# Attention kernel: the sums of two tiles in one run, three buffers of probabilities, one buffer of rounded biases

## What is computed

```python
qkv = (x.reshape(B, S, dim) @ qkv_w + qkv_b)            # x is _gn(x)
attn = jnp.einsum('bqc,bkc->bqk', q * scale, k)
rel_h = jnp.einsum('bhwc,hkc->bhwk', r_q, Rh)
rel_w = jnp.einsum('bhwc,wkc->bhwk', r_q, Rw)
attn = attn + rel_h[..., :, None] + rel_w[..., None, :]  # 2304 x 2304 for each head
out = softmax(attn) @ v
x = x + (out @ proj_w + proj_b)
```

## Time and profile before

| | us |
|---|---|
| median of 3 runs | 7006.76 |
| range of the runs | 7003.55 to 7010.83 |
| the profiled execution, its own time | 7003.42 |
| its span, first to last instruction | 7001.6 |
| PE busy | 6841.4 (98%) |
| DVE busy | 5486.4 (78%) |
| ACT busy | 4650.1 (66%) |
| GpSimd busy | 934.5 (13%) |

### The profile page before, as it was taken

One profiled execution on the slowest core, in us unless ns is written; L12 is line 12 of the kernel. 1 busy time (PEld: TensorE's weight loads), 2 busy tenths in 40 slices (PEclk: granted clock), 3 DMA queues, 4 the chain that ended last, 5 costly groups with the idle time before them and its releaser, 6 DMA issues.

```text
span 7001.6 us, 139199 instructions
## 1 busy us (share of the span) xinstructions
PE 6841.4 (98%) x53600; PEld 4298.1 (61%) x53600; DVE 5486.4 (78%) x10165; ACT 4650.1 (66%) x10033; POOL 934.5 (13%) x967
## 2 busy tenths in 40 slices
PE   7999999999999999999999999999999999999998
PEld 4666666666666666666665666656666566666664
DVE  6887888778887788877888778887787878877883
ACT  2667676666666676666766666667676666766765
POOL 2112010110102110111111111102101121101110
PEclk8999999999999999999999999999999999999999
DMA  5666676666667666666666666766667666666663
GB/s 142 142 148 155 134 150 144 155 154 133 152 133 158 149 138 154 142 162 138 145 143 147 153 142 141 153 146 154 143 139 152 139 159 142 139 148 144 144 145 93
DMA packets 306306, 1013.72 MB, mean 145 GB/s; under 512 B 107440, under 2 KB 196976, under 8 KB 215920
## 3 DMA queue, kind: packets, MB, share of 16 engines
q1 hardware_dynamic: 305648, 1004.81, 64.4%
HBM read 745.26 MB, written 255.69 MB: 143 GB/s over the span
## 4 chain that ended last, share of the span: by engine, by line
PE 93%; DMA 3%; DVE 2%; issue 0%; SPq 0%; ACT 0%; POOL 0%; POOLq 0%; DVEq 0%; ACTq 0%
PE work L791 31%; PE work L782 27%; PE work L861 26%; PE work L807 4%; DMA moving<-rel_scratch 3%; PE work L826 2%; PE work L845 2%; DVE mpart L660 1%; PE work L834 1%; PE work L813 0%; DMA qk_scratch<-back 0%; DVE xb L651 0%; ACT probs L547 0%; DVE stats L610 0%; POOL back L495 0%
## 5 line engine op out<-in xcount | busy, mean ns | idle before, releaser
L660 DVE TENSOR_REDUCE mpart<-work 128x1 f32<-128x512 f32 (+1 forms) x8640 | 5091.4, 631 | 1217.2 <-PE work L791 1196.8
L547 ACT ACTIVATE probs<-work 128x512 f32<-128x512 f32 (+1 forms) x8640 | 4047.8, 557 | 951.4 <-PE work L782 936.8
L782 PE MATMUL work<-moving,keys 113*128 113x512 f32 (+1 forms) x8640 | 3395.8, 394 | 78.8 <-DMA moving<-rel_scratch 73.7
L791 PE MATMUL work<-mkeys,hi 128*128 128x512 f32 (+1 forms) x8640 | 3451.7, 401 | 11.8 <-DVE mpart L660 8.6
L791 PEld LDWEIGHTS work<-mkeys,hi 128*128 128x128 f32 x8640 | 1647.8, 191 | 1152.4 <-DVE mpart L660 866.8
L861 PE MATMUL work<-probs,vall 128*17 128x288 f32 x27648 | 2016.3, 409 | 0.0
L782 PEld LDWEIGHTS work<-moving,keys 113*128 113x128 f32 x8640 | 1645.7, 191 | 534.4 <-ACT probs L547 141.4
L861 PEld LDWEIGHTS work<-probs,vall 128*17 128x17 f32 x27648 | 637.4, 97 | 803.2 <-ACT probs L547 245.0
L480 POOL TENSOR_TENSOR full<-full,hi 128x384 f32<-128x384 f32 x576 | 580.8, 1009 | 1417.0 <-DVE hi L705 1417.0
L530 ACT ACTIVATE full<-work 48x384 f32<-48x384 f32 x576 | 279.3, 486 | 604.5 <-PE work L807 604.5
L535 ACT ACTIVATE full<-work 48x384 f32<-48x384 f32 x576 | 278.9, 484 | 583.6 <-PE work L807 583.6
(11 more groups left out here) (42 smaller groups left out, 649.1 us busy)
## 6 DMA issues: line engine op xcount, KB each, us to landing
moving<-rel_scratch SPq DMA_DIRECT2D x1728, 144.0 KB
moving<-qk_scratch SPq DMA_DIRECT2D x288, 576.0 KB
rel_scratch<-hi SPq DMA_DIRECT2D x192, 432.0 KB, 5.9
rel_scratch<-full SPq DMA_DIRECT2D x192, 432.0 KB, 5.5
moving<-rel_scratch SPq DMA_DIRECT2D x288, 288.0 KB
image<-qk_scratch SPq DMA_DIRECT2D x384, 144.0 KB, 4.2
keys<-qk_scratch SPq DMA_DIRECT2D x192, 288.0 KB, 4.8
qk_scratch<-split_hi SPq DMA_DIRECT2D x144, 192.0 KB, 3.8
```

Of the source, the lines that this page charges most:

```text
L547: act.activation(probs[:, tile % RING, lo:up], bank[:, 0:up - lo], ACT.Exp).then_inc(act_read, 1)
L660: dve.tensor_reduce(mpart[:, u % 2, q, m:m + 1], bank[:, 0:MSPLIT[m][1] - MSPLIT[m][0]], AX.X, ALU.max)\
L782: pe.matmul(bank[:, 0:up - lo], tile_of(keys[0:K_ROWS, u % 2, :], c, third), moving[0:K_ROWS, slot_of(u, third)[0], lo:up], start=True, st ...
L791: pe.matmul(bank[:, 0:up - lo], hi[:, u % 2, q * P:(q + 1) * P], mkeys[:, u % 2, lo:up], start=True, stop=True).then_inc(for_dve, 1)
```

## The change

The sums of tiles are no longer one run at the end of each tile: at the end of every even t PE does those of the two tiles before, one behind the other, and at the end of odd t none. So that the exponentials of a further tile have a place, `probs` has three buffers in place of two. The space comes from `hi`, which has one buffer in place of two. A conversion of `hi` may therefore overwrite columns only after the maxima matmuls that read them; each now waits for the last reduction of those, and the sixth moves from t = 13 after the third reduction to the end of t = 13, ahead of `top`. On SP the store of `hi` moves from t = 13 to t = 14, and that of `full` from t = 14 to t = 15.

```diff
-RING = 2
+RING = 3
...
-        hi = sb("hi", [P, 2, N], F32R)
+        hi = sb("hi", [P, N], F32R)
...
-                    if t == 13 and u + 2 < UNITS:
-                        sp.wait_ge(hi_ready, NB * (u + 3))
-                        rel_store(u + 2, hi[:, (u + 2) % 2, :].bitcast(F32), 0, rel_hi_stored)
                     if t == 14 and 0 <= u + 1 < UNITS:
                         top_load(u + 1, 0)
                     if t == 14 and u + 2 < UNITS:
-                        sp.wait_ge(lo_ready, NB * (u + 3))
-                        rel_store(u + 2, full[:, :], 1, rel_lo_stored)
+                        sp.wait_ge(hi_ready, NB * (u + 3))
+                        rel_store(u + 2, hi[:, :].bitcast(F32), 0, rel_hi_stored)
...
                     if t == 15 and 0 <= u + 1 < UNITS:
                         top_load(u + 1, 1)
+                    if t == 15 and u + 2 < UNITS:
+                        sp.wait_ge(lo_ready, NB * (u + 3))
+                        rel_store(u + 2, full[:, :], 1, rel_lo_stored)
...
                 if r == 0:
                     dve.wait_ge(fullq_in, 32 * (u + 1))
-                    if u >= 2:
-                        dve.wait_ge(rel_hi_stored, 32 * (u - 1))
-                dve.tensor_copy(hi[:, u % 2, cols], full[:, cols]).then_inc(hi_ready, 1)
+                    if u:
+                        dve.wait_ge(rel_hi_stored, 32 * u)
+                if u:
+                    dve.wait_ge(dve_read, place["max", u - 1, 3 * r + 2, MAXB - 1] + 1)
+                dve.tensor_copy(hi[:, cols], full[:, cols]).then_inc(hi_ready, 1)
...
-                        if 8 <= t < 14 and i == 2 and -2 <= u and u + 2 < UNITS:
-                            high(u + 2, t - 8)
+                        if -2 <= u and u + 2 < UNITS:
+                            if 8 <= t < 13 and i == 2:
+                                high(u + 2, t - 8)
+                            if (t, i) == (13, 5):
+                                high(u + 2, 5)
...
-                        if i == SB and 0 < tile <= TILES * UNITS:
+                        if i == SB and t % 2 == 0 and 0 < tile <= TILES * UNITS:
+                            attend(tile - 2)
                             attend(tile - 1)
```

More of the change, by code:

```diff
@@ L479, in low @@
                 pool.wait_ge(hi_ready, NB * u + r + 1)
-                pool.tensor_tensor(full[:, cols], full[:, cols], hi[:, u % 2, cols].bitcast(F32), ALU.subtract)\
+                pool.tensor_tensor(full[:, cols], full[:, cols], hi[:, cols].bitcast(F32), ALU.subtract)\
                     .then_inc(lo_ready, 1)
@@ L790, in fill @@
                         pe.wait_ge(mkeys_in[u % 2], 32 * (u // 2 + 1))
-                    pe.matmul(bank[:, 0:up - lo], hi[:, u % 2, q * P:(q + 1) * P], mkeys[:, u % 2, lo:up],
+                    pe.matmul(bank[:, 0:up - lo], hi[:, q * P:(q + 1) * P], mkeys[:, u % 2, lo:up],
                               start=True, stop=True).then_inc(for_dve, 1)
```

## The result

The changed kernel takes 7193.09 us (median of four runs, 7190.21 to 7196.79). The kernel before takes 7005.4 us (four runs, 7003.55 to 7010.83). The ratio is 1.0268, 95% interval 1.0255 to 1.028. The prediction was 7077 us with a range up to 7160: it foresaw a loss of 74 us, and the loss is 188 us, above the range. The mechanism it names (three banks, DVE late in the first tile of a pair, PE waiting in the second) is there, in pairs 11-12 and 15-16 of plain units to the hundredth of a microsecond. What failed is what it took for pairs with other work in them, above all the projection and value items; and a term that it set at nothing is there.

A forecast was written before the change was run, and what follows sets the result against it. PE, busy for 98%, bounds the kernel; its possible 259 us saving is outweighed by waits for DVE and ACT. Unit terms 40 - 21 - 2 + 38 + 13 + 6 give +74 on 7003: 7077 us, range 6985 to 7160.

The forecast's parts named there:

- The saving on PE: PE over a pair of tiles: 0.30 us saved, nine pairs in 96 units 259 us if nothing else gave way.
- the units with queries and keys: 21 units with query and key items in tiles 1 to 11: ACT holds second tiles, +1.8 us a unit, +38.
- The five pairs from 1 to 10: Tiles 1 to 10, with bias tiles: ACT becomes the ring that holds; between -0.45 and +0.3 us, +0.1 taken.
- The drains win: Rival: weight loads taken ahead hide PE's refill and ACT's latency; each pair 0.12 us better, 6973 us; chance 0.16.
- even: Rival: half of PE's 0.1 us refill after each wait is hidden; 7003 us in the middle; chance 0.13.
- gives DVE the rest that the sums gave: Projection and value items in tiles 12 to 17: their PE time rests DVE; four pairs gain 0.2 to 0.3 each.
- head 3: Seven units with two more DVE statistics per tile: +0.5 us a pair for three pairs, +1.8 a unit, +13.
- pair 13-14: Last conversion moved ahead of the row of maxima, which the transposition awaits: 7.87 us against 7.32, +0.55.
- absorbs what tiles 9 to 14 lose: Eight first units of a stage: a transfer wait in tile 14 covers the losses of those tiles; +0.7 a unit.
- the plain unit: 32 units without extra items: terms 0.17 + 0.55 + 0.43 + 0.1 + 0 make +1.25 us each, 40 in all.
- Costed at nothing: One buffer of rounded biases, three of probabilities, later bias stores: 0 us taken; stores up to 96 us in the range.
- The rival's condition: Late stores make ACT wait at tile 0 from a landing of about 7 us: 1 us a unit, 7173; chance 0.12.

The follow-up runs named there:

- e6: Changed kernel with half of each reduction to a maximum and each exponential left out, bias stores back at tiles 13 and 14: 6813.96 us.
- e9: Changed kernel with half of each reduction to a maximum left out and bias stores back at tiles 13 and 14: 6995.4 us.
- e10: Changed kernel with half of each exponential left out, whole reductions, bias stores back at tiles 13 and 14: 7103.83 us.
- e12: e2 with the projection or value item of tiles 13, 15 and 17 moved behind the tile's last score matmul: 7152.51 us.
- e5: Kernel before with half of each reduction to a maximum and half of each exponential left out: 6947.97 us.
- e7: Changed kernel with the transposition of the row of maxima moved behind the fourth score matmul of tile 14: 7189.79 us.
- e1: Changed kernel with the sums again in one run at the end of every tile, its other changes kept: 7038.21 us.
- e4: Changed kernel, stores late, with half of each reduction to a maximum left out: 7030.48 us.
- e2: Changed kernel with the two bias stores back at the ends of tiles 13 and 14: 7183.66 us.

## Why the prediction was right in sign and wrong in size

**Right.** The saving on PE (0.30 per pair; 0.31 in e6), the length of the double run (2.07; 2.06, though its formula, with 0.253 for the group and not 0.245, gives 2.10), the step between tiles (0.12; 0.13), pairs 15-16 (6.98), 11-12 (7.68) and 17-0 (7.08; 7.10), and the units with queries and keys (+38; +41). The five pairs from 1 to 10 (+0.1; +0.13) are right by a choice between -0.45 and +0.3. That the lags of DVE and ACT hold PE is shown by e9, e10 and e6; that they act through the three banks is read off the timeline, and the number of banks was not varied. *The drains win* and *even* needed PE's refill after a wait to be hidden; it is not, each held maxima matmul is followed by its score matmul only 0.34 us later.

**Wrong sign, 51 us: "gives DVE the rest that the sums gave".** Of the projection and value items in tiles 12 to 17 the prediction said that the four pairs there gain 0.2 to 0.3 each, -21 us in all. They lose 0.30 (15-16), 0.31 (13-14), 0.53 (11-12) and 0.05 (17-0; 0.4 in head 2, whose second tile there is the first with statistics of head 3), and the units of heads 1, 2 and 7 as a whole +30 us. The step asked whether the item brings time, not where in the pair it stands. DVE's lag arises behind the item, in the last reductions of the first tile, and is the same 1.15 us at its end with or without it; the item's own addition is 0.54 us of DVE's time on top; and the second tile's item, second in the ring there, waits for the first tile's fourth reduction. With the item at the seam (e12) pair 15-16 of heads 1 and 2 does gain 0.22 against before, pair 13-14 0.24 and 17-0 0.21, just the "0.2 to 0.3" that was written down; 11-12, whose first tile has no item, gains nothing. The mechanism was right for a place where the item was not.

**Mis-sized, 23 us: head 3.** DVE's two statistics per tile were put at +0.5 a pair for three pairs. Pairs 1-2 to 5-6 of head 3 take 8.94, 8.21 and 8.29 us in place of 7.97, 7.31 and 7.55, that is +0.97, +0.90 and +0.74. DVE over pair 3-4 of unit 51, before:

```profile
3797.01 1.59 DVE L660 TENSOR_REDUCE mpart<-work 128x1 f32<-128x512 f32 x3
...
3804.29 0.67 DVE L660 TENSOR_REDUCE mpart<-work 128x1 f32<-128x512 f32 x1
```

and with the change:

```profile
3907.28 0.42 DVE L660 TENSOR_REDUCE mpart<-work 128x1 f32<-128x256 f32 x1 [0.83 <-PE work L796]
...
3914.58 0.25 DVE L696 RECIPROCAL den<-den 128x18 f32<-128x18 f32 x1
```

Between the two rows of each stand ten reductions and four statistics: 7.28 us before (3797.01 to 3804.29) and 7.30 after (3907.28 to 3914.58). Before, DVE did that without a rest, and PE's pair took as long, 7.31. Now DVE cannot work through the double run, since it holds only three banks (0.83 us idle), and PE waits for all of it afterwards: 8.21. The prediction added what the statistics cost but not that a DVE with no slack pays for its forced rest in full. The larger part of the miss lies further on. Pairs 9-10, 11-12 and 15-16 of head 3, where the steps of the normalisation stand on DVE, were not counted apart and lose 0.7, 0.9 and 1.0. With DVE halved (e9) the unit takes 75.3 us, before 75.5.

**Wrong, 15 us: the transfer in tile 14 of a stage's first unit "absorbs what tiles 9 to 14 lose".** These units lose 2.6 us, not 0.7. Their wait at the start of tile 14 did not shrink with the loss: from the tile's first maxima matmul to its first score matmul there are 4.83 us in the mean of the eight, before 4.15. And the clock falls behind it, which the prediction left out. In unit 48 of the changed kernel:

```profile
3725.86 0.79 PE L787 MATMUL work<-moving,keys 113*128 113x512 f32 x1 [5.28 <-DMA moving<-rel_scratch]
```

The windows view of 3725.80 to 3730.60 has a granted clock of 0.50, the lower of its two levels (1.2 and 2.4 GHz), and the matmuls there follow in 0.43 us (3726.46 to 3726.89) in place of 0.24. Before, the same unit waited 3.48 us and the clock fell as well, for a shorter time. Over tile 14 of the eight units the clock is at this level for 27 us before and 51 after; at 0.43 for 0.24 these 24 us cost some 10, an estimate. (In the whole profile of the kernel before the mean granted clock is 0.989, so it is at the lower level for about 2% of the span, not 1%.) In e6, where the other pairs are shorter, pair 13-14 of these units takes 15.2 us in the median, in e5 12.8. So what starts the transfer seems to move with the tiles around it; its chain, link by link, was not tested.

**Mis-sized, 11 us: the plain unit**, +1.61 in the mean of the plain units in place of +1.25. The medians of its pairs make +1.50; the rest comes from eight single pairs 1-2 and 17-0 that are 0.3 to 1.3 us longer than the others. The largest term is pair 13-14 with 0.13. The timeline of tile 14 in unit 45:

```profile
3518.34 0.36 DVE L707 CAST hi<-full 128x384 fp32r<-128x384 f32 x1
3518.62 0.24 DVE L711 TENSOR_REDUCE mcol<-mpart 128x18 f32<-128x90 f32 x1
3519.01 0.38 PE L818 MATMUL work<-ident,mcol 128*18 128x128 f32 x2 [0.21 <-ACT probs L547]
```

The last reduction of tile 13 ends at 3515.29 + 2.95 = 3518.24 and the conversion begins 0.10 later, since it now waits for that reduction's semaphore; the transposition comes at 3519.01, 0.15 after L711's end. In the prediction both hops were 0.05 to 0.06. The list of waits has 29.1 us for this wait, in 51 units; in this one the profile names ACT instead. Behind the transposition it is 1.78 us to the sums, before 1.81, so the pair ends where this wait puts it; but with the wait taken away (e7) the ring holds the pair at 7.98.

**Costed at nothing, and 10 us here: the late stores.** In 31 of 95 units of the changed kernel ACT's first bias copy starts 0.07 us after the second store has landed; before there were 0.9 to 8.3 us between them, 4.1 in the median. SP and ACT around the end of unit 45, answering to the earlier trace rows:

```profile
3526.08 1.56 SPq L330 DMA_DIRECT2D rel_scratch<-full  x2
```

```profile
3532.96 0.48 ACT L530 ACTIVATE full<-work 48x384 f32<-48x384 f32 x1
```

From issue to copy there are 6.88 us in place of 10.60; the prediction had estimated 6.6. The rival's condition, a landing of about 7 us, is nearly met: 6.8 us here, 6.5 in the median, and copy and landing meet to 0.07 us. Its price, 1 us a unit, is too high: 32 to 35 us in all where nothing else covers it (e1; e4 against e9), 10 us here (e2).

These terms, 51 + 23 + 15 + 11, with 10 in head 8 (items again) and 3 in the units with queries and keys, are the 113 us between 74 and 187.

## What to carry to other kernels

Before two short rests of a trailing engine are merged into one long one, lay out how far it is behind at the end of the first half and how many banks it may be behind: here a run of sums per tile cost PE 0.31 us a pair and spared it 0.5 us of waiting, and only halving the work of the trailing engines, not any order of it, turned that round. Filler work helps such an engine only if it stands at the seam, after the lag has arisen and before the banks are needed again; the same four matmuls cost 0.3 us a pair in front of the lag and gave 0.2 behind it. And after the first wait has been found, ask what stands right under it: removing the wait for the transposition (e7) or ACT's share alone in tiles 12 to 17 (e10) moved nothing.

## What was not expected of the hardware

A full ring is nearly invisible in the profile's list of waits. PE's waits of line L796 for DVE went from 8.6 to 24.1 us, while halving DVE's reductions gave 188 us, 167 of them in the units; the time is in starts that are 0.1 to 0.15 us late, in matmuls recorded as 0.50 us in place of 0.40, and in the distance of 0.34 us behind them.

Halving what a reduction or an exponential reads is worth less than half: the mean reduction of 512 columns takes 683 ns and that of 256 takes 422, the mean exponential goes from 560 to 362 ns. And two reliefs that overlap are not additive: 188 and 80 us apart, 370 together.
